# The end of a two-layer attention kernel: key sums on the matrix engine, an early start of the last projection, and a last part in four pieces

## The chip, the cores and the metric

The kernel runs on one core of a Trainium2 chip. The metric is the device time of one execution in microseconds. The kernel before takes 1591.75 us, the median of 3 runs (1589.45 to 1593.44). The engines are called as the profile calls them: PE (matrix multiply), DVE (vector), ACT (activation functions), POOL (GpSimd) and SP (which only issues DMAs).

## The reference

Two layers over 8 batches of 512 rows and 512 features. The first is a graph attention with 20 keys; it is finished before the part that this change touches. The second, cut to what matters:

```python
h = _sln(hidden, w, ...)                       # layer norm with learned gain and shift
qkv = (h @ Wqkv.T + bqkv)                      # 16 heads of 32 features
energy = jnp.einsum('bhqd,bhkd->bhqk', q, k)
att = jax.nn.softmax(energy, axis=-1) / D ** 0.5
out = jnp.einsum('bhqk,bhkd->bhqd', att, v)
out = out @ Wp.T + bp
h1 = out + hidden
h2 = _sln(h1, w, ...)
return h2 + h1
```

The softmax needs the sum of its exponentials over the keys (called key sum here). Since it is over keys, which lie on partitions, it is a sum across partitions.

## The kernel before

The second layer handles a batch in four units of four heads each; a unit is written (b, c) with b = 0..7 and c = 0..3, so the last two units are (7, 2) and (7, 3). A unit has 16 slots. In a slot PE writes one transposed score block of 128 keys by 512 queries (`scores_t`, L1407) into bank 0 or 1, ACT takes its exponential into the tile `pt` (`exp`, L1169), and PE may overwrite the bank two slots later. Beside it PE makes, in the same slot, the next unit's scores for the row maximum (L1420, with a DVE maximum behind it) and one piece of a projection: three matmuls of 512 columns (L48 to L50, `mm3`), which are the three products of a number split in a high and a low part. In the last unit there is no next unit and no projection, so its slots hold one matmul each.

`pt` holds four key chunks of four heads. The key sum is made in two steps. POOL adds the four chunks (`key_sum`, L1017 and L1022: six additions of 128x1024 for a unit) into `acc`, and PE multiplies `acc` with a tile of ones (`denominators`, L1455, four matmuls), which adds over the partitions and puts the sum on all 32 rows of a head (bank XB = 5). PE multiplies `pt` with the values in `weighted` (L1444, eight matmuls for two key chunks, twice per unit: at slot 14, and at slot 2 of the next unit; bank OB = 4). DVE takes the reciprocal of the sum in four pieces of 128 columns (`reciprocals`, L1295) and multiplies (`quotients`, L1302); ACT adds a bias and splits off the high part (`output_hi`, L1176 and L1179), POOL makes the low part (`output_lo`, L1036, into `ol`). `ol` of all four units is what the output projection of the batch needs (`output`, L48 to L50: 4 tiles of 128 rows by 4 pieces of contraction, one piece for each unit, three matmuls each). For batches 0 to 6 that projection lies in the next batch's slots. For batch 7 it stands after everything else, in banks 6, 7, 0 and 1. Behind it DVE adds the residual (L1381) and makes the statistics, POOL the reciprocal root (L1027, L1031), ACT the normalised tile (L1257), and DVE and POOL finish it (L1390, L1096, L1393); SP stores the four tiles.

The order on each engine is written out by hand; engines wait for each other through counting semaphores. POOL's order matters most here: between key sums it also makes `output_lo` and the results of the batch before (`result`, L1045 to L1049).

Of the kernel before, what the change touches and what calls it, by code (L numbers as in the profile page):

```python
# [847 lines left out]
def attention(nc, t, d):  # L848
# [12 lines left out]
    with ExitStack() as ctx:  # L861
# [70 lines left out]

        def last_tiles():

            return [(v[:, 0, i, :], pt[:, 0, i, :]) for i in range(NT)]
# [72 lines left out]
        def _(pool):  # L1008
# [42 lines left out]
            def batch(b, bpar, more):  # L1051
                later = not first(b)
                for c in range(FC):
                    if not start(b, c):
# [8 lines left out]
                    key_sum(b, c, 0, 1)  # L1063
                    key_sum(b, c, 0, 2)
# [4 lines left out]
                    key_sum(b, c, 1, 0)  # L1069
# [4 lines left out]
                    key_sum(b, c, 1, 1)  # L1074
                    if c == 2:
                        output_lo(b, 1)
# [9 lines left out]
            key_sum(B - 1, FC - 1, 1, 2)  # L1086
            output_lo(B - 1, FC - 1)
# [11 lines left out]
        def _(act):  # L1099
# [56 lines left out]
            def exp(b, c, slot):  # L1156
                G = 4 * b + c
                half, i, k = slot // 8, slot % 8 // 2, slot % 2
                if k == 0 and not start(b, c):
                    if i == 0:  # L1160
                        act.wait_ge(s["pv_done"], 2 * G - 1)
                        act.wait_ge(s["sum_done"], 6 * G + 3 * half - 5)
                    if i == 2:
                        act.wait_ge(s["pv_done"], 2 * G)
                        act.wait_ge(s["sum_done"], 6 * G + 3 * half - 4)
                    if i == 3:
                        act.wait_ge(s["sum_done"], 6 * G + 3 * half - 3)
# [86 lines left out]
            output_hi(B - 1, FC - 1)  # L1254
# [6 lines left out]
        def _(dve):  # L1261
# [26 lines left out]
            def reciprocals(b, c, piece):  # L1288
# [6 lines left out]
                nc.vector.reciprocal(rden[:, c % 2, col], bank[:, XB, col]).then_inc(s["rden_done"], 1)  # L1295
# [77 lines left out]
            for piece in range(4):  # L1373
                reciprocals(B - 1, FC - 1, piece)
            quotients(B - 1, FC - 1)
            hy = last_tiles()
            dve.wait_ge(s["h4_in"], 16)
            for i in range(NT + 2):
                if i < NT:
                    dve.wait_ge(s["pj_ready"], 4 * (B - 1) + i + 1)  # L1380
                    nc.vector.tensor_tensor(hy[i][0], bank[:, (QB, KB, 0, 1)[i], :], hy[i][0], ALU.add).then_inc(s["h1_done"], 1)  # L1381
# [14 lines left out]
        def _(pe):  # L1396
# [37 lines left out]
            def weighted(b, vpar, c, part):  # L1434
# [5 lines left out]
                if c == 0:  # L1440
                    pe.wait_ge(s["v_done"], 4 * b + 2 + 2 * part)
                for i in (2 * part, 2 * part + 1):
# [76 lines left out]

            def piece(b, c, slot, more):  # L1520
# [23 lines left out]
            def batch(b, bpar, more):  # L1544
                for c in range(FC):
                    former = None if start(b, c) else ((b, bpar, c - 1) if c else (b - 1, 1 - bpar, 3))
                    following = c < 3 or more
                    for slot in range(SLOTS):
# [8 lines left out]
                        if slot == 4 and former:  # L1557
                            denominators(former[0], former[2])
# [141 lines left out]
```

## Time and profile before

| | |
|---|---|
| time, median of 3 runs | 1591.75 us |
| time of the profiled execution | 1588.15 us |
| its span, first to last instruction | 1586.4 us |
| PE busy | 1376.4 us (87%) |
| DVE busy | 923.2 us (58%) |
| POOL busy | 899.5 us (57%) |
| ACT busy | 631.1 us (40%) |
| mean granted PE clock | 0.927 |

Busy time is the sum of an engine's instructions; the span is what one execution lasts on the core, and 1.75 us more lie around it. The granted clock is a share of 2.4 GHz; it is 1.0 or 0.5 (1.2 GHz) at any time, and a mean between them says how long each lasted. The last unit's first slot starts at 1525.47 us and the last DVE instruction ends at 1583.85 us.

### The profile page before, as it was taken

The page shows a single profiled execution, that of the slowest core. Times are in us where ns is not written, and L with a number is a line of the kernel's source. Part 1 is how long each engine was busy: PE and PEld are TensorE (multiplying, and loading weights), DVE is VectorE, ACT ScalarE, POOL GpSimd, SP SyncE. Part 2 cuts the span into 40 slices and gives each one's busy share as a digit, 9 for nine tenths or more (in the row PEclk, how much of TensorE's full clock was granted, in tenths as well). Part 3 has the DMA queues.
Part 4 walks back from the last instruction along what each step waited for, and adds up shares of the span by engine and source line. Part 5 has one row for each costly group of instructions (what it writes and reads, how often), then busy time and mean ns, then how long its engine had stood idle before and what let it go on. Part 6 is the DMA issues. An engine that isn't in the chain of part 4 may idle for free.

```text
span 1586.4 us, 19843 instructions
## 1 busy us (share of the span) xinstructions
PE 1376.4 (87%) x5988; PEld 873.2 (55%) x5988; DVE 923.2 (58%) x1494; ACT 631.1 (40%) x1090; POOL 899.5 (57%) x568
## 2 busy tenths in 40 slices
PE   6986998898898995279999999999999999999974
PEld 3644665665665663155565656555556555656532
DVE  2541665665664755136566757576667566666744
ACT  0231323324334232315454545545545445454551
POOL 1004434545545524316466958778769578687793
PEclk9997899999998987579999999999999999999977
DMA  9454213333323212724224425344344244253310
GB/s 297 177 174 129 83 65 132 136 113 135 125 106 153 86 60 106 265 73 109 73 61 127 114 61 147 94 107 108 87 127 111 62 127 111 70 143 89 104 46 27
DMA packets 107192, 179.41 MB, mean 113 GB/s; under 512 B 41312, under 2 KB 50848, under 8 KB 101840
## 3 DMA queue, kind: packets, MB, share of 16 engines
q1 hardware_dynamic: 94976, 143.92, 29.5%
q10 hardware_dynamic: 12112, 34.24, 7.2%
q8 instruction: 49, 0.80, 0.2%
q14 instruction: 55, 0.45, 0.1%
HBM read 81.06 MB, written 46.17 MB: 80 GB/s over the span
## 4 chain that ended last, share of the span: by engine, by line
PE 19%; POOL 17%; issue 8%; DVE 8%; ACT 3%; DMA 1%; SPq 1%; ACTq 1%; POOLq 0%; DVEq 0%
POOL acc L1022 7%; PE a_bank L1444 4%; PE a_bank L1407 4%; DVE rden L1295 4%; POOL acc L1017 3%; PE a_bank L1420 3%; PE a_bank L48 2%; PE a_bank L49 2%; PE a_bank L50 2%; DVE mx L1277 2%; PE a_bank L1455 2%; POOL h L1046 2%; POOL tn L1045 2%; ACT pt L1169 1%; DMA pt<-in_wp_t 1%
## 5 line engine op out<-in xcount | busy, mean ns | idle before, releaser
L1277 DVE TENSOR_REDUCE mx<-a_bank 128x1 f32<-128x512 f32 x512 | 341.9, 674 | 275.0 <-PE a_bank L1420 273.3
L1169 ACT ACTIVATE pt<-a_bank 128x512 f32<-128x512 f32 x512 | 301.9, 597 | 380.6 <-PE a_bank L1407 354.7
L1022 POOL TENSOR_TENSOR acc<-acc,pt 128x1024 f32<-128x1024 f32 x128 | 305.1, 2384 | 18.1 <-ACT pt L1169 9.9
L1407 PE MATMUL a_bank<-sq_stack,sk_stack 98*128 98x512 f32 x512 | 227.6, 447 | 31.1 <-ACT pt L1169 15.1
L1420 PE MATMUL a_bank<-sk_stack,sq_stack 96*128 96x512 f32 x512 | 220.0, 433 | 21.0 <-DVE mx L1277 19.7
L1017 POOL TENSOR_TENSOR acc<-pt 128x1024 f32<-128x1024 f32 x64 | 152.7, 2386 | 117.4 <-PE a_bank L1455 77.4
L1407 PEld LDWEIGHTS a_bank<-sq_stack,sk_stack 98*128 98x128 f32 x512 | 98.6, 193 | 158.3 <-issue 97.7
L774 PE MATMUL g_bank<-m,sf 128*128 128x320 f32 x512 | 161.9, 461 | 1.9 <-issue 1.9
L1420 PEld LDWEIGHTS a_bank<-sk_stack,sq_stack 96*128 96x128 f32 x512 | 99.9, 195 | 68.7 <-DVE mx L1277 54.6
L1295 DVE RECIPROCAL rden<-a_bank 128x128 f32<-128x128 f32 x128 | 120.1, 942 | 20.2 <-PE a_bank L1455 20.2
L48 PE MATMUL a_bank<-hh,wqkh 128*128 128x512 f32 x256 | 104.4, 408 | 27.5 <-DVE wqkl L1365 27.5
L1444 PE MATMUL a_bank<-pt,v 128*32 128x512 f32 x1024 | 126.6, 613 | 0.7 <-ACT pt L1169 0.7
L774 PEld LDWEIGHTS g_bank<-m,sf 128*128 128x128 f32 x512 | 97.0, 199 | 45.0 <-issue 15.7
L49 PE MATMUL a_bank<-hl,wqkh 128*128 128x512 f32 x256 | 103.5, 404 | 0.0
L50 PE MATMUL a_bank<-hh,wqkl 128*128 128x512 f32 x256 | 102.7, 401 | 0.0
L494 POOL TENSOR_TENSOR e<-e,cadd 128x640 f32<-128x640 f32 x32 | 49.4, 1543 | 92.0 <-DVE e L667 92.0
L479 POOL TENSOR_TENSOR xl<-xraw,xh 128x512 fp32r<-128x512 f32 x32 | 40.1, 1267 | 70.0 <-ACT xh L550 61.8
L689 DVE TENSOR_TENSOR wtl<-g_bank,wth 80x512 fp32r<-80x512 f32 x64 | 43.3, 685 | 57.8 <-ACT wth L583 57.4
L48 PE MATMUL g_bank<-wth,vdiag 80*128 80x512 f32 x64 | 40.1, 627 | 41.1 <-DVE wtl L689 41.0
L667 DVE TENSOR_TENSOR e<-g_bank,mask 128x640 f32<-128x640 f32 x32 | 26.4, 824 | 84.5 <-PE g_bank L776 84.5
L48 PEld LDWEIGHTS a_bank<-hh,wqkh 128*128 128x128 f32 x256 | 49.9, 195 | 39.3 <-DVE wqkl L1365 27.9
L566 ACT ACTIVATE ln<-xn,nmr,rstd 128x512 f32<-128x512 f32 x32 | 23.4, 802 | 120.7 <-DVE nmr L719 120.7
(164 smaller groups left out, 2540.6 us busy)
## 6 DMA issues: line engine op xcount, KB each, us to landing
sq_stack<-qh SPq DMA_DIRECT2D x256, 64.0 KB, 2.0
sk_stack<-kh SPq DMA_DIRECT2D x256, 64.0 KB, 2.3
m_rows<-mout SPq DMA_DIRECT2D x8, 1280.0 KB, 5.0
m<-m_rows SPq DMA_DIRECT2D x8, 1280.0 KB, 5.7
xraw<-in_x_t SPq DMA_DIRECT2D x8, 1024.0 KB, 7.5
xn<-in_x SPq DMA_DIRECT2D x8, 1024.0 KB, 6.8
h_rows<-xn ACTq DMA_DIRECT2D x8, 1024.0 KB, 3.9
t_rows<-houth SPq DMA_DIRECT2D x8, 1024.0 KB, 3.9
```

Source lines behind the costliest of these rows:

```text
L48: nc.tensor.matmul(out, ah, bh, start=start, stop=False)
L49: nc.tensor.matmul(out, ah, bl, start=False, stop=False)
L50: return nc.tensor.matmul(out, al, bh, start=False, stop=stop)
L774: nc.tensor.matmul(out, sf2[:, par, f, i * P:(i + 1) * P], m[:, f, dr, :], start=f == 0, stop=False)
L1017: nc.gpsimd.tensor_tensor(acc[:, two, :], pt[:, 0, two, :], pt[:, 1, two, :], ALU.add).then_inc(s["sum_done"], 1)
L1022: nc.gpsimd.tensor_tensor(acc[:, two, :], acc[:, two, :], pt[:, step + 1, two, :], ALU.add).then_inc(s["sum_done"], 1)
L1169: nc.scalar.activation(pt[:, i, 2 * half + k, :], bank[:, k, :], ACT.Exp).then_inc(s["exp_done"], 1)
L1277: nc.vector.reduce_max(mx[:, half, k, n:n + 1], bank[:, 2 + e % 2, :], AX).then_inc(s["emax_done"], 1)
L1295: nc.vector.reciprocal(rden[:, c % 2, col], bank[:, XB, col]).then_inc(s["rden_done"], 1)
L1407: nc.tensor.matmul(bank[:, k, :], sk[0:3 * DH + 2, c % 2, j, i * P:(i + 1) * P], sq[0:3 * DH + 2, c % 2, j, :], start=True, stop=True).the ...
L1420: nc.tensor.matmul(bank[:, 2 + e % 2, :], sq[0:3 * DH, c % 2, j, n * P:(n + 1) * P], sk[0:3 * DH, c % 2, j, :], start=True, stop=True).the ...
L1444: last = nc.tensor.matmul(bank[DH * j:DH * j + DH, OB, :], v[:, vpar, i, (HC * c + j) * DH:(HC * c + j + 1) * DH], pt[:, i, j, :], start=i ...
```

## The change

There are three parts, and all lie in units (7, 2) and (7, 3) and in what follows them.

1. For the last two units POOL makes no key sums. PE multiplies every chunk of `pt` with the ones, right ahead of each `weighted` part: eight matmuls of 32 rows by 512 for each part, four parts. The sum of (7, 2) goes to bank KB = 7, that of (7, 3) to XB. The waits of `exp` for those sums go too.
2. Of the last projection the pieces of units (7, 0), (7, 1) and (7, 2), twelve of sixteen, are put in slots 3 to 14 of the last unit, in banks 6, 2, 3 and 7. Four pieces, those of (7, 3), are left for the end.
3. What follows the last `weighted` goes in pieces of 128 columns (128 output rows): reciprocal, product, the two activations and the low part, and each piece releases one tile's last three matmuls.

```diff
+        def final(b, c):
+            return isinstance(b, int) and b == B - 1 and c >= 2
+        END = (QB, 2, 3, KB)
...
-                    key_sum(b, c, 0, 0)
+                    if not final(b, c):
+                        key_sum(b, c, 0, 0)
...
-            key_sum(B - 1, FC - 1, 1, 2)
-            output_lo(B - 1, FC - 1)
+            for p in range(NT):
+                col = slice(p * P, (p + 1) * P)
+                pool.wait_ge(s["ob_done"], 4 * B + p)
+                nc.gpsimd.tensor_tensor(ol[:, FC - 1, col], rden[:, 1, col], oh[:, FC - 1, col].bitcast(F32),
+                                        ALU.subtract).then_inc(s["ol_done"], 1)
...
-            output_hi(B - 1, FC - 1)
+            for p in range(NT):
+                n, col = 4 * B + p, slice(p * P, (p + 1) * P)
+                act.wait_ge(s["o_done"], n)
+                nc.scalar.activation(oh[:, FC - 1, col], rden[:, 1, col], ACT.Identity,
+                                     bias=bvs[:, FC - 1:FC]).then_inc(s["oh_done"], 1)
+                act.wait_ge(s["oh_done"], n)
+                nc.scalar.activation(rden[:, 1, col], rden[:, 1, col], ACT.Identity,
+                                     bias=bvs[:, FC - 1:FC]).then_inc(s["ob_done"], 1)
...
-            for piece in range(4):
-                reciprocals(B - 1, FC - 1, piece)
-            quotients(B - 1, FC - 1)
+            for p in range(NT):
+                col = slice(p * P, (p + 1) * P)
+                reciprocals(B - 1, FC - 1, p)
+                if p == 0:
+                    dve.wait_ge(s["pv_done"], 8 * B)
+                dve.wait_ge(s["rden_done"], 16 * (B - 1) + 12 + p + 1)
+                nc.vector.scalar_tensor_tensor(rden[:, 1, col], bank[:, OB, col], float(D) ** -0.5, rden[:, 1, col],
+                                               ALU.mult, ALU.mult).then_inc(s["o_done"], 1)
...
+                if final(b, c):
...
+                    for i in (2 * part, 2 * part + 1):
+                        for j in range(HC):
+                            last = nc.tensor.matmul(bank[DH * j:DH * j + DH, KB if c == 2 else XB, :], ones32[:, :],
+                                                    pt[:, i, j, :], start=i == 0, stop=i == NT - 1)
+                    if part == 1:
+                        last.then_inc(s["den_ready"], 1)
...
+            early = {3: (0, 0), 4: (1, 0), 5: (2, 0), 6: (0, 1), 7: (1, 1), 8: (2, 1), 9: (3, 0), 10: (3, 1),
+                     11: (0, 2), 12: (1, 2), 13: (2, 2), 14: (3, 2)}
...
+                if final(b, c) and c == 3 and slot in early:
+                    i, f = early[slot]
+                    if f == 0:
+                        pe.wait_ge(*((s["h1_done"], 4 * b), (s["emax_done"], SLOTS * FC * B), (s["emax_done"], SLOTS * FC * B),
+                                     (s["rden_done"], 4 * (4 * b + c)))[i])
+                    output(b, i, END[i], f)
...
-            denominators(B - 1, FC - 1)
-            pe.wait_ge(s["h1_done"], 4 * (B - 1))
             for i in range(NT):
-                for f in range(FC):
-                    output(B - 1, i, (QB, KB, 0, 1)[i], f)
+                pe.wait_ge(s["ol_done"], 4 * B + i)
+                output(B - 1, i, END[i], FC - 1)
```

The order on PE in the last unit. This is the kernel before, from slot 3 of unit (7, 3) on; L1407 is a slot's score block, L1455 the key sum of (7, 2) from `acc`, L1444 the first `weighted` part of (7, 3):

```order
L1407 MATMUL a_bank<-sq_stack,sk_stack 128x512 [waits exp_done] x2
L1455 MATMUL a_bank<-acc,ones 32x512 [waits sh_lo,sum_done]
L1455 MATMUL a_bank<-acc,ones 32x512 x3
L1407 MATMUL a_bank<-sq_stack,sk_stack 128x512 [waits exp_done] x3
L1407 MATMUL a_bank<-sq_stack,sk_stack 128x512 [waits exp_done,shrow_lo,shrow_hi]
L1407 MATMUL a_bank<-sq_stack,sk_stack 128x512 [waits exp_done] x6
L1444 MATMUL a_bank<-pt,v 32x512 [waits o_done,exp_done]
```

The changed kernel on PE, from slot 10 to the first part of the key sums and the weighted sum of (7, 3); L1435 is now the score block, L48 to L50 a projection piece, L1478 the ones-matmuls, L1484 `weighted`:

```order
L48 MATMUL a_bank<-wph,oh 128x512 [waits ol_done]
L49 MATMUL a_bank<-wpl,oh 128x512
L50 MATMUL a_bank<-wph,ol 128x512
L1435 MATMUL a_bank<-sq_stack,sk_stack 128x512 [waits exp_done]
L48 MATMUL a_bank<-wph,oh 128x512
L49 MATMUL a_bank<-wpl,oh 128x512
L50 MATMUL a_bank<-wph,ol 128x512
L1435 MATMUL a_bank<-sq_stack,sk_stack 128x512 [waits exp_done]
L48 MATMUL a_bank<-wph,oh 128x512
L49 MATMUL a_bank<-wpl,oh 128x512
L50 MATMUL a_bank<-wph,ol 128x512
```

Each slot from 3 to 14 now holds four matmuls where it held one, and the first piece above, in slot 11, waits for `ol_done`, the low part of unit (7, 2).

DVE at the end of the kernel before, from the last unit's reciprocals to the first residual:

```order
L1295 RECIPROCAL rden<-a_bank 128x128 [waits ol_done,den_ready]
L1295 RECIPROCAL rden<-a_bank 128x128 x3
L1302 SCALAR_TENSOR_TENSOR rden<-a_bank,rden 128x512 [waits rden_done,pv_done]
L1381 TENSOR_TENSOR v<-a_bank,v 128x512 [waits pj_ready,h4_in]
L1315 BN_STATS stat<-v 128x6 [waits h1_done]
```

The same place in the changed kernel (L1317 the reciprocal, L1402 the product of 128 columns, L1409 the residual):

```order
L1317 RECIPROCAL rden<-a_bank 128x128 [waits ol_done,den_ready]
L1402 SCALAR_TENSOR_TENSOR rden<-a_bank,rden 128x128 [waits rden_done,pv_done]
L1317 RECIPROCAL rden<-a_bank 128x128
L1402 SCALAR_TENSOR_TENSOR rden<-a_bank,rden 128x128 [waits rden_done]
L1317 RECIPROCAL rden<-a_bank 128x128
L1402 SCALAR_TENSOR_TENSOR rden<-a_bank,rden 128x128 [waits rden_done]
L1317 RECIPROCAL rden<-a_bank 128x128
L1402 SCALAR_TENSOR_TENSOR rden<-a_bank,rden 128x128 [waits rden_done]
L1409 TENSOR_TENSOR v<-a_bank,v 128x512 [waits pj_ready,h4_in]
```

Reciprocals and products alternate now, and all eight stand ahead of the first residual in DVE's queue.

## Rows read from the trace of the kernel before

**Rows 1.** Busy time of PE, PEld, DVE, ACT, POOL; then granted clock, DMA.

```profile
1522.30:1584.00 61.70, 36.96 (x149) 17.70 (x149) 26.34 (x48) 19.86 (x34) 39.72 (x31) 0.76 0.09 30
```

**Rows 2.** The chain that ended last, from 1530 us: start, us, what.

```profile
1530.50 2.34 POOL acc L1022
...
1550.20 2.35 POOL acc L1022
...
1552.59 1.11 PE a_bank L1455 x8
...
1553.73 3.40 DVE rden L1295 x4
...
1557.22 0.70 DVE rden L1302
...
1557.95 0.73 ACT oh L1176
...
1559.50 1.27 POOL ol L1036
```

**Rows 3.** Timeline of PE, units (7, 2) and (7, 3): start, us, instruction, idle before.

```profile
1519.68 0.47 PE L1407 MATMUL a_bank<-sq_stack,sk_stack 98*128 98x512 f32 x1
...
1520.92 0.39 PE L1407 MATMUL a_bank<-sq_stack,sk_stack 98*128 98x512 f32 x1
...
1523.04 1.92 PE L1444 MATMUL a_bank<-pt,v 128*32 128x512 f32 x16
...
1529.33 0.73 PE L1407 MATMUL a_bank<-sq_stack,sk_stack 98*128 98x512 f32 x2
1532.89 1.55 PE L1455 MATMUL a_bank<-acc,ones 128*32 128x512 f32 x8 [2.83 <-POOL acc L1022]
...
1542.51 3.64 PE L1444 MATMUL a_bank<-pt,v 128*32 128x512 f32 x16
...
1547.56 1.92 PE L1444 MATMUL a_bank<-pt,v 128*32 128x512 f32 x16 [0.69 <-ACT pt L1169]
```

**Rows 4.** Stretches as in Rows 1: PE waits, and what follows them.

```profile
1071.60:1074.00 2.40, 0.07 (x2) 0.04 (x1) 0.09 (x1) 0.00 (x0) 2.32 (x2) 1.00 0.80 229
1074.00:1080.00 6.00, 6.00 (x34) 3.49 (x35) 3.25 (x5) 2.64 (x5) 0.94 (x1) 1.00 0.55 140
1287.40:1290.00 2.60, 0.05 (x1) 0.08 (x1) 0.00 (x0) 0.00 (x0) 2.52 (x2) 1.00 0.76 218
1291.10:1294.40 3.30, 3.30 (x10) 2.42 (x9) 1.68 (x3) 0.95 (x3) 0.00 (x0) 0.50 0.69 188
1510.10:1512.90 2.80, 0.04 (x1) 0.00 (x0) 2.80 (x5) 1.25 (x3) 2.66 (x3) 0.99 0.17 64
1513.00:1519.60 6.60, 6.51 (x15) 4.91 (x16) 3.79 (x6) 2.22 (x4) 6.46 (x5) 0.50 0.17 46
...
1533.40:1546.90 13.50, 11.97 (x35) 3.68 (x27) 4.08 (x5) 6.92 (x12) 13.07 (x8) 0.50 0.19 58
```

**Rows 5.** Timeline of DVE after the last projection has begun.

```profile
1562.57 0.69 DVE L1381 TENSOR_TENSOR v<-a_bank,v 128x512 f32<-128x512 f32 x1 [4.66 <-PE a_bank L50]
...
1564.32 0.14 DVE L1322 TENSOR_SCALAR stat<-stat 128x1 f32<-128x1 f32 x1
...
1568.77 0.69 DVE L1381 TENSOR_TENSOR v<-a_bank,v 128x512 f32<-128x512 f32 x1 [0.83 <-PE a_bank L50]
...
1583.16 0.69 DVE L1393 TENSOR_TENSOR v<-v,pt 128x512 f32<-128x512 f32 x1
```

**Rows 6.** Groups by line and form: xcount, busy us, mean ns, idle before.

```profile
L1169 ACT ACTIVATE pt<-a_bank 128x512 f32<-128x512 f32 x512 | 301.9, 597 | 380.6 <-PE a_bank L1407 354.7 <-POOL acc L1022 15.1 <-issue 7.2
L152 ACT ACTIVATE ident<-ident_raw 128x128 fp32r<-128x128 f32 x1 | 0.3, 310 | 3.0 <-DMA bbias<-in_b_bias 3.0
L1285 DVE SCALAR_TENSOR_TENSOR sht<-a_bank,sht 8x128 fp32r<-8x128 f32 x64 | 17.4, 272 | 7.6 <-ACT sht L1151 7.6
L1022 POOL TENSOR_TENSOR acc<-acc,pt 128x1024 f32<-128x1024 f32 x128 | 305.1, 2384 | 18.1 <-ACT pt L1169 9.9
```

More of the change, by code:

```diff
@@ L1053, in batch @@
                 for c in range(FC):
-                    if not start(b, c):
+                    if not start(b, c) and not final(b, c - 1):
                         key_sum(*(ahead(b, c, -1) if c else (b - 1, 3)), 1, 2)
@@ L1059, in batch @@
                         result(b - 1, 2 * c - 3)
-                    key_sum(b, c, 0, 0)
+                    if not final(b, c):
+                        key_sum(b, c, 0, 0)
                     if later and c in (1, 2):
                         result(b - 1, 2 * c - 2)
-                    key_sum(b, c, 0, 1)
-                    key_sum(b, c, 0, 2)
+                    if not final(b, c):
+                        key_sum(b, c, 0, 1)
+                        key_sum(b, c, 0, 2)
                     if c == 0 and later:
@@ L1068, in batch @@
                         output_lo(b, 2)
-                    key_sum(b, c, 1, 0)
+                    if not final(b, c):
+                        key_sum(b, c, 1, 0)
                     if c == 2:
@@ L1073, in batch @@
                         rsqrt(b - 1, 2 * c - 1)
-                    key_sum(b, c, 1, 1)
+                    if not final(b, c):
+                        key_sum(b, c, 1, 1)
                     if c == 2:
@@ L1161, in exp @@
                         act.wait_ge(s["pv_done"], 2 * G - 1)
-                        act.wait_ge(s["sum_done"], 6 * G + 3 * half - 5)
                     if i == 2:
                         act.wait_ge(s["pv_done"], 2 * G)
+                    if i == 0 and not final(b, c - 1):
+                        act.wait_ge(s["sum_done"], 6 * G + 3 * half - 5)
+                    if i == 2 and not final(b, c - 1):
                         act.wait_ge(s["sum_done"], 6 * G + 3 * half - 4)
-                    if i == 3:
+                    if i == 3 and not final(b, c - 1):
                         act.wait_ge(s["sum_done"], 6 * G + 3 * half - 3)
@@ L1294, in reciprocals @@
                         dve.wait_ge(s["ol_done"], G - 1)
-                nc.vector.reciprocal(rden[:, c % 2, col], bank[:, XB, col]).then_inc(s["rden_done"], 1)
+                nc.vector.reciprocal(rden[:, c % 2, col], bank[:, KB if final(b, c) and c == 2 else XB, col]
+                                     ).then_inc(s["rden_done"], 1)
             def quotients(b, c):
@@ L1380, in _ @@
                     dve.wait_ge(s["pj_ready"], 4 * (B - 1) + i + 1)
-                    nc.vector.tensor_tensor(hy[i][0], bank[:, (QB, KB, 0, 1)[i], :], hy[i][0], ALU.add).then_inc(s["h1_done"], 1)
+                    nc.vector.tensor_tensor(hy[i][0], bank[:, END[i], :], hy[i][0], ALU.add).then_inc(s["h1_done"], 1)
                     statistics(B - 1, i, hy[i][0])
@@ L1441, in weighted @@
                     pe.wait_ge(s["v_done"], 4 * b + 2 + 2 * part)
+                if final(b, c):
+                    if part == 0 and c == 2:
+                        pe.wait_ge(s["h1_done"], 4 * b - 1)
+                    if part == 0 and c == 3:
+                        pe.wait_ge(s["sh_lo"], 2 * FC * B)
+                        pe.wait_ge(s["rden_done"], 4 * (G - 1))
+                    for i in (2 * part, 2 * part + 1):
[4 more added lines that the diff above has]
+                        last.then_inc(s["den_ready"], 1)
                 for i in (2 * part, 2 * part + 1):
@@ L1556, in batch @@
                             weighted(*former, 1)
-                        if slot == 4 and former:
+                        if slot == 4 and former and not final(b, c - 1):
                             denominators(former[0], former[2])
```

## The prediction, made before the changed kernel was run

> **What bounds the end now.** The change touches nothing ahead of the end of unit (7, 2), so I read only the last 63 us. First the stretch from 1522.3 us, where the two kernels part, to the last DVE instruction: POOL is busy 39.72 of 61.70 us, PE 36.96, DVE 26.34 and ACT 19.86 [rows 1]. No engine is full, so a chain decides. The chain of waits says which: from 1530.50 to 1552.55 us it is POOL alone, addition after addition of key sums, with the batch's other POOL work between them; then the sum on PE (1.11 us), four reciprocals (3.40), the product (0.70), two activations (1557.95 to 1559.43), the low part (1.27), and at 1560.82 the first matmul that could finish a tile [rows 2]. PE had done the last `weighted` by 1549.48 and stands still for 3.1 us until the sum is there; at 1530.06 it had stood still for 2.83 us for the sum of (7, 2) [rows 3]. Then comes a tail of DVE: the first residual starts at 1562.57, the third at 1568.77, the last instruction ends at 1583.85 [rows 5].
>
> So the time from 1522.3 us is POOL's chain, a serial hand-over of 13.1 us (1549.48 to 1562.57), and a tail of 21.3 us.
>
> **What the change takes away.** Twelve POOL additions of 2.38 us [rows 6], 28.6 us, leave the queue, nine of them (21.4) in this stretch; eight `acc` matmuls leave PE. POOL keeps some 18 us of work for 62 us [rows 1, 6] and no longer bounds. What is late next is PE, whose queue I replay in order at the full clock. Four blocks are what matters.
>
> (a) *To slot 3 of the last unit.* Each `weighted` part took 1.86 us at full clock (1.92 with its drain) for eight matmuls that fill 32 of 128 columns [rows 3]. The ones-matmuls have the same form and moving data, so eight cost 1.86 again. Bounds: nothing, if they overlapped `weighted` wholly (eight more instructions of one form in one queue; the row shows no such slack), and 3.64 at the half clock [rows 3]. I take 1.86. Two such blocks lie ahead of slot 3, which moves from 1529.33 to 1533.05. The exponential of slot 15 comes later, but waits beside the blocks.
>
> (b) *Slots 3 to 10.* A slot with five matmuls took 1.24 us at full clock (1519.68 to 1520.92) [rows 3], 0.248 each. Four are 0.99. Slot s + 2 needs the exponential of slot s: 0.5 for the matmul and 0.6 on ACT [rows 6], 1.2 in two slots of 1.98, so PE bounds and not ACT. Eight slots are 7.9 us; slot 11's score block starts at 1540.95.
>
> (c) *A new stall in slot 11.* Its piece waits for the low part of unit (7, 2), which ACT begins only behind the exponential of slot 10. That slot's matmul starts at 1539.97; + 0.5 + 0.6 + hand-over = 1541.15; two activations 1.5, low part 1.27, hand-overs 0.1 [rows 2]: 1544.0. PE has nothing from 1541.2 on: 2.8 us idle. Behind the waiting piece stand slots 12 to 14 and both last `weighted` parts, and ACT waits for those slots.
>
> (d) *To the end of the last `weighted`.* Three matmuls and three slots, 0.7 + 2.97 = 3.7: 1547.7. Ones and `weighted` 3.72: 1551.4. Slot 15, its exponential and hand-over 1.2 [rows 3, 6]: 1552.6. Ones and `weighted` 3.72: X = 1556.35. Before it was 1549.48, so PE's part costs 6.9 us more.
>
> (e) *From X to the first residual.* The ones-matmuls end 1.9 us before X, so the first reciprocal is done. Then DVE has four products and three reciprocals in its queue ahead of the first residual. A reciprocal is 0.85 back to back (3.40 for four [rows 2]), 0.95 alone here. A product of 128 columns is not in the trace: between 0.27 (8x128 [rows 6]) and 0.70 (128x512 [rows 2]); I take 0.3, nearest to the 128-column row. 4 x 0.3 + 3 x 0.9 = 3.9, with hand-over X + 4.0. Tile 0 is ready by then: product 0.3, two activations of 128 columns (0.31 each [rows 6], at most 0.73 [rows 2]), low part 0.45 (the line through 1.27 at 512 columns and 2.38 at 1024; at most 1.27), three matmuls 1.0, or 1.7 at the half clock: X + 2.6 to X + 3.3. The other tiles follow every 1.2 us, sooner than DVE can take them. All costs of pieces but the product's are hidden behind DVE's queue; with the product at its upper bound 1.7 us are lost. So 13.1 us of hand-over become 4.0: 9.1 us saved.
>
> (f) *The tail.* Before, the third tile came from PE 6.2 us after the first [rows 5]. Now it is DVE that sets it: a tile's residual and statistics take 1.9 (1562.57 to 1564.46 [rows 5]), two tiles 3.85. From the third residual on everything is as before, 15.08 us [rows 5]. The tail is 18.9 in place of 21.3: 2.4 saved.
>
> **Sum at full clock:** + 6.9 - 9.1 - 2.4 = - 4.6 us.
>
> **The clock.** PE's idle stretches are what this sum has not priced. After 2.8 us of idle at 1510.1 the clock was 0.50 for 6.6 us of dense work; after 2.6 at 1287.4 it was 0.50 for 3.3; after 2.4 at 1071.6 it stayed 1.00; after the 2.83 at 1530.1 it was 0.50 for 13.5 us, of which 11.97 busy, in lone score matmuls with waits between [rows 3, 4]. The stall in (c) is 2.8, so I expect a fall. Each us of low clock in PE-bound work costs 0.5. Dense work follows, so I take a low stretch of 3.4 us: 1.7 lost. Both ends: 0 and 3.3 (6.6 us low). Before, a low clock in the last unit cost nothing, since POOL bounded.
>
> The Trainium skill, TensorE: Matmul & The Clock Gate, section Loop structure matters more than you think, says that a loop which waits between its matmul bursts brings PE back to the slow clock. By that rule the stall of (c) always costs and the sum with it is the forecast; by the 2.4 us row alone it might not, and the sum is the 4.6.
>
> **Forecast:** - 4.6 + 1.7 = - 2.9 us. The profiled execution took 1588.15 (span 1586.4 and 1.75 around it), 3.6 below the median; a difference carries over: 1591.75 - 2.9 = 1588.9 us, a span near 1583.5 in an execution like the profiled one.
>
> **Rivals.**
> - *No fall of the clock.* The stall is a little shorter than I count, or straddles as that of 2.4 us did. - 4.6, and up to 0.4 more if slot 15's wait hides in (a): 1587.1. For it: one of the four stretches. Against: the three others, each 2.6 or longer.
> - *Long low clock after the stall.* As at 1513.0 [rows 4], 6.6 us: - 4.6 + 3.3 = - 1.3, 1590.4. If the product also costs its upper bound, 0.4 slower, 1592.2. Either reads as no change.
> - *Slower: the last unit runs at the half clock.* The clock falls in the sparse slots 15, 0, 1 and 2 or is low as it is before, and stays low through slots 3 to 14, as it did for 13.5 us [rows 4]. PE now bounds there, with 7.9 + 3.7 us of work that doubles: - 4.6 + 11.6 = + 7.0, 1598.8. It decides from 9.2 us of low clock on, where the gain is gone. Against: that stretch had waits in every slot, while four matmuls a slot are dense work, and dense work brought the clock back in 3.3 and 6.6 us.
> - *The change doesn't do what it says*: POOL's chain could still be last if `output_lo` of (7, 2) were behind late results. With 18 us of work left in 62 [rows 1, 6], POOL is idle when that low part comes; no chance of its own.
>
> **Chances.** Forecast 0.42, no fall 0.35, long low 0.12, slower 0.09, others 0.02. What a measurement can tell is 0.3%, 4.8 us. The no-fall case reaches it in half of its share, the forecast in a sixth, with the error of a median of a few runs: faster 0.27. Slower 0.10, no change that can be told 0.63. The range: the low end 1585.0 is the no-fall case less 2 for the error of the replay and of medians. The high end 1594.0 takes in the long low clock with the dear product and the same error; beyond it lies most of the slower case. The forecast's own range is 1586.5 to 1591.3.
>
> **What would show it.** Right: no L1022 after 1505 us; ones-matmuls 1.9 us per part; a slot of about 1.0 us in the last unit at clock 1.0; an idle stretch of 2.8 us in front of slot 11's piece, released by POOL's low part, and a clock of 0.50 behind it; the last `weighted` ending 6 to 9 us later than 1549.5; the first residual 4 us after it; DVE without waits for PE from there on. Wrong: ones-matmuls that cost other than `weighted`; slots set by ACT; a first residual that waits for PE or POOL; a low clock ahead of slot 10; a tail that is not 18.9 us.

## The result: 7.65 us faster, where 2.9 were forecast

The changed kernel takes 1581.80 us (median of 11 runs, 1577.84 to 1589.21), the kernel before 1589.45 (11 runs, 1585.98 to 1595.05; the 1591.75 from which I had worked was a median of three). The ratio is 0.995, 95% interval 0.993 to 0.9969: faster by 5 to 11 us. The direction was right. The size was not: the forecast was 1588.9, with a range from 1585.0 to 1594.0.

The profiled execution took 1580.23 us. Its page, with the busy time of the engines and three of the groups:

```profile
span 1578.3 us, 19927 instructions
...
PE 1372.0 (87%) x6036; PEld 872.2 (55%) x6036; DVE 923.1 (58%) x1497; ACT 633.7 (40%) x1096; POOL 872.0 (55%) x559
...
L1028 POOL TENSOR_TENSOR acc<-acc,pt 128x1024 f32<-128x1024 f32 x120 | 286.1, 2384 | 17.4 <-ACT pt L1184 9.8
...
L1023 POOL TENSOR_TENSOR acc<-pt 128x1024 f32<-128x1024 f32 x60 | 143.3, 2388 | 120.4 <-PE a_bank L1495 79.9
```

Eight additions of L1028 (L1022 before, [rows 6]) and four of L1023 are gone, and POOL is busy 27.5 us less. POOL's busy time isn't the gain; the gain is read from the end of the span. The timeline of PE in units (7, 2) and (7, 3), to be read beside [rows 3] (start, us, instruction, idle before it):

```profile
1519.57 1.92 PE L1478 MATMUL a_bank<-pt,ones 128*32 128x512 f32 x16
1521.31 1.90 PE L1484 MATMUL a_bank<-pt,v 128*32 128x512 f32 x16
...
1528.84 0.50 PE L1435 MATMUL a_bank<-sq_stack,sk_stack 98*128 98x512 f32 x1
1529.88 0.40 PE L1435 MATMUL a_bank<-sq_stack,sk_stack 98*128 98x512 f32 x1
...
1535.47 0.40 PE L1435 MATMUL a_bank<-sq_stack,sk_stack 98*128 98x512 f32 x1
...
1536.41 0.39 PE L1435 MATMUL a_bank<-sq_stack,sk_stack 98*128 98x512 f32 x1
1539.26 0.61 PE L48 MATMUL a_bank<-wph,oh 128*128 128x512 f32 x1 [2.46 <-POOL ol L1042]
...
1549.25 1.92 PE L1478 MATMUL a_bank<-pt,ones 128*32 128x512 f32 x16 [0.69 <-ACT pt L1184]
1550.99 1.90 PE L1484 MATMUL a_bank<-pt,v 128*32 128x512 f32 x16
1554.80 0.47 PE L48 MATMUL a_bank<-wph,oh 128*128 128x512 f32 x1 [1.90 <-POOL ol L1099]
```

The reader sees the new ones block (L1478) ahead of `weighted` (L1484), slots of one score matmul and three of the projection, 0.93 us apart, and in slot 11 the new stall, released by POOL's low part of (7, 2). The granted clock through it, as windows with the columns of [rows 1]:

```profile
1519.50:1536.80 17.30, 17.07 (x104) 8.98 (x103) 7.34 (x14) 11.16 (x20) 7.02 (x7) 1.00 0.19 62
1536.90:1539.20 2.30, 0.00 (x0) 0.00 (x0) 0.00 (x0) 1.42 (x3) 1.26 (x1) 1.00 0.00 0
1539.50:1542.80 3.30, 3.30 (x9) 2.52 (x9) 0.00 (x0) 0.60 (x1) 0.00 (x0) 0.50 0.00 0
1542.90:1554.00 11.10, 9.30 (x72) 3.08 (x71) 2.00 (x3) 2.47 (x5) 0.00 (x0) 1.00 0.01 1
1557.20:1560.00 2.80, 2.80 (x6) 1.64 (x6) 2.63 (x8) 0.85 (x3) 1.20 (x3) 0.50 0.00 0
```

PE is full up to slot 10, empty for 2.3 us, and then full at half the clock for 3.3 us. The chain of waits through the stall (start, us, what):

```profile
1535.91 0.60 ACT pt L1184
1536.51 0.62 ACT oh L1191
1537.14 0.73 ACT rden L1194
...
1537.94 1.27 POOL ol L1042
1539.26 0.61 PE a_bank L48
```

POOL's additions of key sums, which filled this stretch of the chain before [rows 2], have gone, and one low part is left. After the last `weighted` part DVE alone sets the pace up to the third residual, to be read beside [rows 5]:

```profile
1552.96 0.29 DVE L1402 SCALAR_TENSOR_TENSOR rden<-a_bank,rden 128x128 f32<-128x128 f32 x1 [0.76 <-PE a_bank L1484]
...
1554.15 0.29 DVE L1402 SCALAR_TENSOR_TENSOR rden<-a_bank,rden 128x128 f32<-128x128 f32 x1
...
1556.73 0.68 DVE L1409 TENSOR_TENSOR v<-a_bank,v 128x512 f32<-128x512 f32 x1
...
1560.31 0.68 DVE L1409 TENSOR_TENSOR v<-a_bank,v 128x512 f32<-128x512 f32 x1
...
1574.86 0.69 DVE L1421 TENSOR_TENSOR v<-v,pt 128x512 f32<-128x512 f32 x1
```

No residual (L1409) waits for PE any more. From such timelines I split every profile in the same way. F is the start of the first ones or `weighted` block in slot 14 of unit (7, 2); X the end of the last `weighted` part; R1 and R3 the starts of the first and third residual; E the end of the last DVE instruction. F to E is called the end stretch below. All in us:

| kernel | F at | F to X | X to R1 | R1 to R3 | R3 to E | end stretch |
|---|---|---|---|---|---|---|
| before | 1523.04 | 26.44 | 13.09 | 6.20 | 15.08 | 60.81 |
| before, second profile (`e5_same`) | 1522.63 | 26.77 | 13.51 | 7.26 | 15.08 | 62.62 |
| changed | 1519.57 | 33.32 | 3.84 | 3.58 | 15.24 | 55.98 |
| changed, second profile (`e9_changed_again`) | 1526.28 | 33.34 | 3.84 | 3.58 | 15.25 | 56.01 |
| `e1_ones` | 1521.34 | 27.52 | 6.58 | 6.98 | 15.08 | 56.16 |
| `e2_pieces` | 1524.86 | 26.77 | 9.28 | 4.83 | 15.25 | 56.13 |
| `e3_no_early` | 1523.45 | 28.33 | 3.84 | 4.61 | 15.26 | 52.04 |
| `e4_no_stall` | 1521.80 | 29.29 | 3.85 | 3.58 | 15.24 | 51.96 |
| `e6_tail` | 1523.68 | 34.63 | 3.84 | 3.58 | 11.65 | 53.70 |
| `e10_half_again` | 1523.26 | 25.65 | 3.84 | 3.59 | 15.24 | 48.32 |
| `e8_best` | 1526.11 | 24.77 | 3.85 | 3.58 | 11.64 | 43.84 |
| `e11_best_no_early` | 1523.80 | 25.93 | 3.85 | 4.60 | 11.46 | 45.84 |

The column F at has to be read with care. It lies between 1519.57 and 1526.28 us, though the instructions ahead of it are the same but for POOL's key sums of (7, 2), and the two ends of the range are the same kernel twice. One profile's span is therefore no measure of this change, and the end stretch is. Each end stretch here is of one execution; the kernel before and the changed one have two.

### The profile page after: what moved, and what is told of

The parts are those of the page before. It is cut to its first block, busy times and chain, and to the rows that moved or that the text cites. A ratio compares the mean times of both kernels' runs of the same rounds, so it can differ in the third digit from the quotient of the medians.

```text
span 1578.3 us, 19927 instructions
## 1 busy us (share of the span) xinstructions
PE 1372.0 (87%) x6036; PEld 872.2 (55%) x6036; DVE 923.1 (58%) x1497; ACT 633.7 (40%) x1096; POOL 872.0 (55%) x559
## 4 chain that ended last, share of the span: by engine, by line
PE 20%; POOL 16%; DVE 8%; issue 8%; ACT 3%; DMA 2%; SPq 1%; ACTq 1%; POOLq 0%; DVEq 0%
POOL acc L1028 7%; PE a_bank L1484 4%; PE a_bank L1435 4%; DVE rden L1317 4%; POOL acc L1023 3%; PE a_bank L1448 3%; PE a_bank L48 2%; PE a_bank L49 2%; PE a_bank L50 2%; DVE mx L1299 2%; POOL h L1052 2%; POOL tn L1051 2%; PE a_bank L1495 1%; ACT pt L1184 1%; DMA pt<-in_wp_t 1%
## 5 line engine op out<-in xcount | busy, mean ns | idle before, releaser
L1028 POOL TENSOR_TENSOR acc<-acc,pt 128x1024 f32<-128x1024 f32 x120 | 286.1, 2384 | 17.4 <-ACT pt L1184 9.8
L1435 PE MATMUL a_bank<-sq_stack,sk_stack 98*128 98x512 f32 x512 | 225.7, 441 | 31.2 <-ACT pt L1184 15.7
L1023 POOL TENSOR_TENSOR acc<-pt 128x1024 f32<-128x1024 f32 x60 | 143.3, 2388 | 120.4 <-PE a_bank L1495 79.9
L1435 PEld LDWEIGHTS a_bank<-sq_stack,sk_stack 98*128 98x128 f32 x512 | 97.9, 191 | 153.3 <-issue 96.3
L774 PE MATMUL g_bank<-m,sf 128*128 128x320 f32 x512 | 158.5, 454 | 1.9 <-issue 1.9
L1317 DVE RECIPROCAL rden<-a_bank 128x128 f32<-128x128 f32 x128 | 120.3, 942 | 19.9 <-PE a_bank L1478 19.8
L48 PE MATMUL a_bank<-hh,wqkh 128*128 128x512 f32 x256 | 104.1, 407 | 27.4 <-DVE wqkl L1388 27.4
L1484 PE MATMUL a_bank<-pt,v 128*32 128x512 f32 x1024 | 124.6, 605 | 0.0
L50 PE MATMUL a_bank<-hh,wqkl 128*128 128x512 f32 x256 | 102.5, 400 | 0.0
L48 PE MATMUL g_bank<-wth,vdiag 80*128 80x512 f32 x64 | 40.5, 633 | 40.4 <-DVE wtl L689 40.2
L48 PEld LDWEIGHTS a_bank<-hh,wqkh 128*128 128x128 f32 x256 | 50.0, 195 | 39.1 <-DVE wqkl L1388 27.8
```

The lines of the kernel that those rows point to most:

```text
L48: nc.tensor.matmul(out, ah, bh, start=start, stop=False)
L50: return nc.tensor.matmul(out, al, bh, start=False, stop=stop)
L774: nc.tensor.matmul(out, sf2[:, par, f, i * P:(i + 1) * P], m[:, f, dr, :], start=f == 0, stop=False)
L1023: nc.gpsimd.tensor_tensor(acc[:, two, :], pt[:, 0, two, :], pt[:, 1, two, :], ALU.add).then_inc(s["sum_done"], 1)
L1028: nc.gpsimd.tensor_tensor(acc[:, two, :], acc[:, two, :], pt[:, step + 1, two, :], ALU.add).then_inc(s["sum_done"], 1)
L1317: nc.vector.reciprocal(rden[:, c % 2, col], bank[:, KB if final(b, c) and c == 2 else XB, col]).then_inc(s["rden_done"], 1)
```

## Experiments

Two theories stood against each other after the result. A: the gain arises in the end stretch, as the prediction has it, with terms mis-sized. B: a good part of it arises ahead of F, where F had come 3.5 us earlier in the changed kernel's profile.

### Each part alone

`e1_ones` has part 1 only (ones-matmuls on every chunk), on the changed kernel:

```diff
-            early = {3: (0, 0), 4: (1, 0), ... 14: (3, 2)}
+            early = {}
 # ACT, POOL and DVE end with whole output_hi, output_lo, reciprocals, quotients again
 # PE: all sixteen pieces behind the last weighted
```

> Part 1 alone: ones-matmuls for the last two units, the projection whole at the end, the hand-over in whole tiles. The measure is the end stretch: from the first block of weighted or ones-matmuls in slot 14 of (7,2) to the end of the last DVE instruction; 60.8 us in the kernel before, 56.0 in the changed one. Theory A (a replay of the queues: POOL's chain goes, slots are then set by the matmul-exponential loop, 0.62 us each, and the early projection fills PE beyond what the slots leave free): the last weighted ends 26 to 28 us into the stretch in place of 33.3 in the changed kernel, the hand-over takes 6.3, the tail 21.3; end stretch 54 to 56, that is 5 to 7 us under before. Theory B (the early projection carries the gain): this alone saves no more than 2 us, end stretch 58 or more.

Measured: 1584.06 us against 1589.71 for the kernel before measured beside it (ratio 0.9966, interval 0.9942 to 0.999); end stretch 56.16. It falls just above the 54 to 56 that was expected. The ones save by themselves 4.65 us of the 60.81. R1 follows X by 6.58 instead of 13.09, since the wait of 3.11 us for POOL's sum [rows 2, 3] is gone, and the reciprocals start 1.65 us ahead of X (1547.21) and not 4.25 behind it.

`e2_pieces` has part 3 only, on the kernel before: POOL makes the key sums as before, and the end goes in pieces of 128 columns.

```diff
-            output_hi(B - 1, FC - 1)
+            for p in range(NT):
 # as in the change, on ACT, POOL and DVE; PE's piece f == 3 of tile i waits for ol_done 4 * B + i
```

> Part 3 alone, on the kernel before: key sums by POOL, projection at the end, the hand-over in pieces of 128 columns. Both theories: the last weighted ends at 26.4 us as before, 3.1 us wait for the key sum, four reciprocals and products ahead of the first residual. Hand-over from the key sum on 4.8 in place of 8.9 us, tail still set by PE: end stretch 56 to 57.5, 3.5 to 4.5 us under before. If the pieces were worth something only with the early projection: 60 or more.

Measured: 1585.25 (0.997, 0.9949 to 0.9991); end stretch 56.13, as expected. So parts 1 and 3 save 4.7 us each against the first profile of before, and together they should be able to save nearly twice that. The changed kernel, which has both, saves 4.83.

### Without the early start

`e3_no_early` leaves out part 2 alone:

```diff
-            early = {3: (0, 0), 4: (1, 0), ... 14: (3, 2)}
+            early = {}
...
+            pe.wait_ge(s["h1_done"], 4 * (B - 1))
             for i in range(NT):
-                pe.wait_ge(s["ol_done"], 4 * B + i)
-                output(B - 1, i, END[i], FC - 1)
+                for f in range(FC):
+                    if f == FC - 1:
+                        pe.wait_ge(s["ol_done"], 4 * B + i)
+                    output(B - 1, i, END[i], f)
```

> Parts 1 and 3 without part 2: no projection piece in the last unit's slots, all sixteen behind the last weighted, tile by tile. Theory A: slots of 0.62 us, no stall in slot 11, last weighted ends 26 to 28 us into the stretch; hand-over 4.0; the third tile is ready 8.8 us after the last weighted and not 7.7: end stretch 26.5 + 8.8 + 15.1 = 50.4, plus up to 3 us for a low clock in the tail: 50.5 to 53.5, 2.5 to 5.5 us faster than the changed kernel. Theory B: the early pieces save what they do at the end, 12 x 0.7 = 8.3 us: end stretch 58 or more, slower than the changed kernel.

Measured: 1579.35 (0.9934, 0.9914 to 0.9955); end stretch 52.04, 3.9 less than the changed kernel. Part 2, the early start of the projection, makes the end slower. The medians point the same way (2.4 us), but their intervals overlap, so the profiles carry this. PE's timeline of this kernel shows the price of thin slots beside it:

```profile
1535.13 3.49 PE L1435 MATMUL a_bank<-sq_stack,sk_stack 98*128 98x512 f32 x6 [0.19 <-ACT pt L1184]
...
1541.18 3.64 PE L1478 MATMUL a_bank<-pt,ones 128*32 128x512 f32 x16
...
1548.14 1.92 PE L1478 MATMUL a_bank<-pt,ones 128*32 128x512 f32 x16 [0.69 <-ACT pt L1184]
```

Here x6 are the score matmuls of six slots. They take 3.5 us, 0.6 each, which is the exponential's 597 ns [rows 6]; four matmuls in a slot take 0.93. But the ones block at 1541.18 takes 3.64 where the later one takes 1.92: the clock was low.

```profile
1539.20:1545.90 6.70, 5.93 (x26) 1.76 (x30) 0.00 (x0) 2.29 (x5) 1.27 (x1) 0.52 0.00 0
```

### Without the stall

`e4_no_stall` keeps all three parts and moves ACT's two activations of (7, 2) four slots up, so that the low part is there before slot 11:

```diff
-                            if c == 3:
+                            if c == 3 and more:
                                 output_hi(b, 2)
+                        if slot == 6 and c == 3 and not more:
+                            output_hi(b, 2)
```

> The changed kernel with the activations of (7,2) behind the exponential of slot 6 in place of slot 10, so that its low part is there when slot 11's piece wants it. Theory A: no idle stretch of 2.8 us in slot 11, and so no low clock behind it: end stretch 56.0 - 2.5 - 1.6 = 52 us (53.5 if the clock falls elsewhere). Rival (the stall is hidden behind ACT or DVE anyway): 55.5 to 56, the wait only moves to another slot.

Measured: 1579.04 (0.9938, 0.9916 to 0.9959); end stretch 51.96. The stall and its low clock cost the changed kernel 4.02 us, against 4.5 forecast (2.8 idle and 1.7 of clock). The window from F to behind X (at 1551.09) shows PE busy for 29.42 of 32.30 us and the clock whole:

```profile
1521.70:1554.00 32.30, 29.42 (x187) 14.28 (x186) 11.14 (x21) 16.73 (x31) 9.17 (x10) 1.00 0.11 34
```

It ends where `e3_no_early` ends: twelve early pieces, with the stall cured, are worth nothing. F to X is 0.96 us longer than without them, and R1 to R3 1.03 us shorter. What they save after X lay behind DVE's queue but for that 1.03. What they cost ahead of X is time in the slots: from slot 3's score matmul to the ones block of slot 14 it is 11.62 us (1531.08 to 1542.70) where `e3_no_early` takes 8.42 (1532.76 to 1541.18), 3.2 more. The two blocks behind it take 2.2 us longer in `e3_no_early`, at its low clock, and that is why only 1.0 is left.

### The same kernels again

`e5_same` is the kernel before, unchanged.

> The kernel before, unchanged: what the measurement shows between two equal kernels, and a second profile of it. The stretch ahead of the last units started within 5.3 us of each other in six kernels with the same code there. Theory A (those differences, and about 3 us of the 7.7 by which the medians of before and after differ, are the spread of one execution to the next, where the clock falls in other places): ratio 1.000 within 0.003, span anywhere in 1581 to 1590, end stretch 60 to 63. Theory B (the change also makes the part ahead of slot 14 of (7,2) faster): this kernel reaches that slot later than the changed one in every profile, at 1523 us or more, and its stretch from slot 8 to slot 14 of (7,2) lasts 9.7 to 10 us as in the two kernels with POOL's key sums, in place of the 8.5 of the four with ones-matmuls.

Measured: 1589.80 (1.0009, 0.9992 to 1.0027), as theory A has it. From slot 8 to F it took 9.64 us (1512.99 to 1522.63), close to theory B's 9.7 to 10. Its end stretch is 62.62, 1.81 more than in the first profile. F to X and X to R1 hold 0.75 of that, R1 to R3 1.06. The reason for most of it stands in a window on the projection, here and then in the first profile of the kernel before:

```profile
1560.30:1566.50 6.20, 5.34 (x13) 4.18 (x14) 1.78 (x5) 0.70 (x1) 1.54 (x3) 0.50 0.01 3
```

```profile
1560.70:1564.00 3.30, 3.18 (x8) 2.51 (x9) 1.39 (x2) 0.00 (x0) 0.06 (x1) 0.50 0.02 5
```

The low clock lasted 6.2 us instead of 3.3, and the residuals, which wait for PE in this kernel, came later:

```profile
1562.91 0.69 DVE L1381 TENSOR_TENSOR v<-a_bank,v 128x512 f32<-128x512 f32 x1 [4.66 <-PE a_bank L50]
...
1570.17 0.69 DVE L1381 TENSOR_TENSOR v<-a_bank,v 128x512 f32<-128x512 f32 x1 [0.84 <-PE a_bank L50]
```

`e9_changed_again` is the changed kernel, unchanged.

> The changed kernel, unchanged, measured again beside the next two. Theory A (what its first comparison shows beyond the end stretch is spread): ratio between 0.9945 and 0.998, that is 3 to 9 us, its end stretch 54.3 to 57.5 by where the clock falls. Theory B (about 3 us are gained ahead of the end stretch): ratio 0.995 or less again, and slot 14 of (7,2) reached before 1521 us again.

Measured: 1581.78 (0.9953, 0.9936 to 0.997), end stretch 56.01. F was at 1526.28 instead of 1519.57, and the ratio is the same, so an early F is no mark of the changed kernel. What is left for theory B is the stretch from slot 8 to F. It took 9.64 to 9.95 us in all three profiles with POOL's key sums of (7, 2) (both of before, `e2_pieces`), and 8.5 in six and 9.5 to 9.7 in three of the nine with ones-matmuls. The means are 0.9 us apart; with three profiles against nine that can be chance, and no run decides it. The stall in slot 11 and the fall behind it are there again:

```profile
1543.40:1545.90 2.50, 0.12 (x1) 0.00 (x0) 0.00 (x0) 1.64 (x3) 1.24 (x1) 1.00 0.00 0
1546.60:1549.80 3.20, 3.20 (x9) 2.52 (x8) 0.00 (x0) 0.99 (x2) 0.00 (x0) 0.50 0.02 5
```

### The tail

`e6_tail` lets POOL do its addition for tile i - 1 right behind the root of tile i, where it was tile i - 2:

```diff
-            for i in range(NT + 2):
+            for i in range(NT + 1):
...
-                if i >= 2:
-                    y = hy[i - 2][0]
-                    pool.wait_ge(s["ln_done"], 4 * (B - 1) + i - 1)
+                if i >= 1:
+                    y = hy[i - 1][0]
+                    pool.wait_ge(s["ln_done"], 4 * (B - 1) + i)
```

> The changed kernel with POOL's additions in the tail one place earlier: tile 0's behind the root of tile 1 in place of tile 2, and so on. If the waits of DVE for POOL (two of 1.99 us in the tail) are on the path: from the third residual to the end 11.3 to 13.3 us in place of 15.2, end stretch 52.5 to 54. If the two engines then run into each other (the last product took 1.66 us beside POOL's additions and 0.69 without): 14 to 15, end stretch 55 or more.

Measured: 1580.92 (0.9943, 0.9926 to 0.996); end stretch 53.70. R3 to E falls from 15.24 to 11.65. The 3.6 us are not all seen in the end stretch, because in this execution the low clock after the stall of slot 11 lasted 6.2 us, from 1543.4 to 1549.6 by the length of its matmuls (0.63 instead of 0.40), where it had lasted 3.4: F to X is 34.63 instead of 33.32. The medians show little of the 3.6: 1580.92 against 1581.80 and 1581.78 for the changed kernel, differences that the intervals do not tell from 3.6 or from nothing.

### Better versions

`e7_half` starts six pieces early instead of twelve, one in every second slot, none of which needs (7, 2). That unit's activations go to slot 14, its first piece behind slot 15's score matmul, and the other nine pieces behind the last `weighted`.

```diff
-            early = {3: (0, 0), 4: (1, 0), ... 14: (3, 2)}
+            early = {3: (0, 0), 5: (0, 1), 7: (1, 0), 9: (1, 1), 11: (2, 0), 13: (2, 1)}
```

> Six of the twelve early pieces, in every second slot from 3 to 13; one piece behind slot 15's score block; the other five behind the last weighted and between the four last parts; the activations of (7,2) behind the exponential of slot 14. Theory A (a slot leaves PE 0.4 us free, so three matmuls in two slots cost nothing, and the hand-over of 2.2 us holds three pieces): last weighted 25 to 27 us into the stretch, hand-over and tail as in the changed kernel (22.7): end stretch 47.5 to 50, 6 to 8 us under the changed kernel and 2 to 4 under the one without early pieces. Rival (PE's clock falls in the thinner slots, 0.74 us a slot and 3.6 us blocks at half clock): 51 to 53.

Measured: 1575.74, the median of all 7 executions, or 1575.36 without the one that took 4452.93 us (0.991, 0.9886 to 0.9935). The profile is of that one and cannot be split. It is told of under the hardware below. `e10_half_again` is the same kernel, measured again.

> The kernel with six early pieces in every second slot, again, since one execution of its first measurement (the profiled one) ran with PE at a fraction of its speed from end to end. As then: end stretch 47.5 to 50 by theory A, 51 to 53 if the clock falls in the thin slots; ratio 0.990 to 0.993.

Measured: 1576.01 (6 runs; 0.9915, 0.9894 to 0.9936), the same time again, and an end stretch of 48.32. Theory A had 47.5 to 50. F to X is 25.65, the shortest so far and less than before the change, though it holds the ones blocks and half of the pieces.

`e8_best` adds the tail of `e6_tail`, lets slot 15's score matmul go ahead of the ones block of slot 14 in the last unit, puts ACT's two activations in slot 15, and moves the first piece of (7, 2) behind the last `weighted`.

```diff
-                        if slot == 14:
+                        if slot == (15 if final(b, c) and c == 3 else 14):
                             weighted(b, bpar, c, 0)
```

> As the one with six early pieces, and in addition: the first ones and weighted block of (7,3) behind slot 15's score block in place of slot 14's, so that the exponential of slot 15 runs beside it; the activations of (7,2) behind slot 15; POOL's additions in the tail one place earlier. Theory A: 0.7 us less for the block's place and 2 to 3.5 for the tail: end stretch 44 to 47.5, 13 to 17 us under the kernel before. If the tail gives nothing: 47 to 49.

Measured: 1570.05 (6 runs, 1567.66 to 1574.62; 0.988, 0.9856 to 0.9904), the fastest: 19 us under the kernel before measured beside it (1589.47). The end stretch is 43.84, just under the 44 to 47.5 that was expected. PE's timeline has matmuls in pairs and the two last blocks without a wait between:

```profile
1535.39 0.50 PE L1437 MATMUL a_bank<-sq_stack,sk_stack 98*128 98x512 f32 x1
...
1536.42 0.65 PE L1437 MATMUL a_bank<-sq_stack,sk_stack 98*128 98x512 f32 x2
...
1543.81 1.92 PE L1480 MATMUL a_bank<-pt,ones 128*32 128x512 f32 x16
...
1547.27 1.90 PE L1480 MATMUL a_bank<-pt,ones 128*32 128x512 f32 x16
1548.98 1.90 PE L1486 MATMUL a_bank<-pt,v 128*32 128x512 f32 x16
```

```profile
1526.10:1551.00 24.90, 24.67 (x167) 10.35 (x167) 8.31 (x16) 14.46 (x26) 8.31 (x8) 1.00 0.14 44
```

PE is busy 24.67 of 24.90 us at the full clock. `e11_best_no_early` asks whether the six pieces do anything: it is `e8_best` with `early = {}` and all pieces at the end.

> The best kernel so far (end stretch 43.8) without any piece in the last unit's slots; all sixteen behind the last weighted, tile by tile. What early pieces are worth once the slots are not PE's bound: theory A: a slot with one matmul is no shorter than one with two and a half (0.62 to 0.67), the third tile comes 8.8 us after the last weighted in place of 7.4: end stretch 44.5 to 46, 0.7 to 2 us worse; if the clock falls in the thin slots and PE's 48 matmuls at the end run at half clock, 48 to 51. Rival (early pieces worth nothing): 43.5 to 44.

Measured: 1576.22 (6 runs; 0.9913, 0.9888 to 0.9937), end stretch 45.84, 2.0 more. Its slots are thin again, and the clock fell in them:

```profile
1537.50:1543.90 6.40, 6.21 (x18) 2.09 (x22) 0.00 (x0) 5.18 (x9) 0.18 (x1) 0.51 0.11 38
```

Here the early pieces help, by 1.2 us from F to X and by 1.0 from R1 to R3. The medians say 6 us, but the two intervals overlap (0.9856 to 0.9904, 0.9888 to 0.9937), and the 2.0 is from one profile of each. That the pieces help is likely; how much stays open.

## Why the direction was right and the size was not

By the prediction's own steps:

**(a) to slot 3.** 9.27 us (1519.57 to 1528.84), forecast 10.01 (1523.04 to 1533.05). A ones block costs what a `weighted` part does: 1.74 from its start to the next block's, 1.92 with its drain. I had taken 1.86. Of the wait of 0.68 us for an exponential that stood in this stretch before, 0.23 are left; I had allowed that only in a rival. 0.74 too much.

**(b) slots 3 to 10.** 7.57 (1528.84 to 1536.41), 1.04 for the first slot and 0.93 to 0.94 for the others, forecast 7.9. I had divided a slot of five matmuls by five, 0.248, but a matmul in a row takes 0.233; the first of that slot had taken 0.32. 0.33 too much.

**(c) the stall.** It is there, in slot 11, released by POOL's low part and named ahead of time. From the score matmul of slot 10 (1535.47) to PE's next start (1539.26) it took 3.79, forecast 4.03; idle 2.46, forecast 2.8. 0.24 too much.

**The clock.** It fell in all three profiles of kernels with this stall (changed, `e9_changed_again`, `e6_tail`), for 3.4, 3.4 and 6.2 us of PE's work. The first two are the forecast's case: F to X is 4.03 us longer than in `e4_no_stall`, of which the idle is 2.46 and the clock about 1.6, forecast 1.7. `e6_tail` is the rival of a long low clock, and its F to X is 1.3 us longer again. The rival without a fall had 0.35, and none of the three shows it. The Trainium skill says that a loop which waits for a DMA between its matmuls brings the slow clock back (TensorE: Matmul & The Clock Gate, Loop structure matters more than you think). The windows agree in that the clock was 0.50 behind each of the three waits of 2.46 us in slot 11; the page's example waits 8 us each time, and behind the 2.4 us at 1071.6 us of the kernel before the clock stayed 1.00 [rows 4].

**(d) to the last `weighted`.** 13.63 from the end of the stall to X, forecast 12.35 + 1.7. 0.42 too much. With (a) to (c), F to X is 33.32 instead of 35.0: 6.9 us more than before, where 8.6 were forecast with the clock in. That the prediction has 6.9 too, at the full clock, is chance: the measured 6.9 holds 1.6 us of clock, which the 1.7 us too much in (a) to (d) make up for.

**(e) the hand-over.** 3.84, forecast 4.0. Product of 128 columns 0.29 (forecast 0.3), low part 0.45 (0.45), activation 0.40 (0.31, hidden). That DVE's queue hides all the costs of pieces but the product's was right.

**(f) the tail.** 18.82 (3.58 + 15.24), forecast 18.9 (3.85 + 15.08): a tile's residual and statistics take 1.79 and not 1.9, and the rest is 0.16 longer.

**The sum** of the end stretch is 60.81 - 55.98 = 4.83 against the first profile of before, forecast 2.9: the 1.9 us are 1.7 of (a) to (d), every one on the same side, and 0.2 of (e) and (f).

**The step that failed** is the term that I put at nothing, together with the reading of the kernel before from one execution. I wrote that before, a low clock in the last unit cost nothing, since POOL bounded. That holds for the unit but not for the projection behind it. The 13.1 us of hand-over and the 6.2 us from the first to the third residual, which (e) and (f) take away, hold a low clock whose length I took as fixed. PE enters there from a wait of 3.31 us for POOL's low part, at the low clock, and DVE waits for its matmuls:

```profile
1560.82 0.80 PE L48 MATMUL a_bank<-wph,oh 128*128 128x512 f32 x1 [3.31 <-POOL ol L1036]
```

In that execution it was 3.3 us. `e5_same` shows 6.2 and an end stretch 1.8 us longer. The changed kernel's projection also falls to 0.50 (1557.2 to 1560.0), but its residuals no longer wait for PE and R1 to R3 is 3.58 in both profiles. So against the one profile the change saves 4.8 us, against the other 6.6. What I let carry over was the smaller of the two. The changed kernel has a low clock of two lengths as well, behind its stall: by `e6_tail` the long one would add 1.3 us and bring the range to 3.5 to 6.6.

**The rest.** The medians differ by 7.65 us, and by 7.5 going by `e9_changed_again`'s ratio; the end stretches by 4.8 and 6.6. The 1 to 4 us between are inside the interval (0.9936 to 0.997 is 4.8 to 10.2 us) and inside the scatter of F, and remain open: no run located them. Of the 7.1 us by which the forecast missed the median, 2.3 are the old median of three runs, 1.9 the mis-sized terms, and the remaining 2.9 hold the low clock in the projection of before, up to 1.8, and what stays open.

Every execution's mean granted clock is on record, and it bears on this. Twice its distance from 1.0, times the span, is the time at the low clock. It is 231 us in the mean of the 73 executions of the kernel before that stand beside the experiments, and 214 and 216 us in the two sets of the changed one. The end stretches alone have 30 and 33 us of it before (0.75 of 60.81, 0.74 of 62.62) and 19 and 16 after (0.83 of 55.98, 0.86 of 56.01). So most of the 16 us of low clock that the change removes lie in the end stretch, and little is left for a gain ahead of F.

**What the prediction did not ask** is what each part is worth. By one profile each, parts 1 and 3 save 4.7 and part 2 loses 3.9: four matmuls in a slot make PE the bound (0.93 against 0.6), and a piece stands in the queue 2.5 us before its low part is there. This was written in (b) and (c) as a cost, but I had not set it against what part 2 saves, which (e) already said is hidden.

## What to carry to other kernels

Work that is moved into another loop's slots should fill what the bounding engine leaves, and no more. Here ACT's 0.6 us a slot leaves room for three matmuls in every second slot. With nothing beside the one score matmul the clock fell, and four in a slot make PE the bound. Before moving work ahead, look for the latest product that it reads, and place it behind that; `e4_no_stall` and `e10_half_again` gained 4.0 and 7.7 us by order alone. And measure the end that a change touches from a mark just ahead of it, in two profiles of each kernel. Here that mark shifted by 7 us between two executions of one kernel, and the terms worked out here are smaller.

## What the runs showed of the hardware

- **The clock fell around every stall of some 3 us, and stayed low for one of two times.** In all 12 profiles of the table PE stands idle for 2.94 to 2.97 us ahead of slot 8 of unit (7, 2). Read in windows of 0.1 us, the granted clock is then 0.50 for 3.4 us in six of them and for 6.8 or 6.9 in the other six. When it fell tells the two apart: in the six long ones it fell 0.2 to 1.2 us before PE started again, in the six short ones when PE started or up to 1.5 us later. The three stalls in slot 11 divide in the same way (3.4 us twice, 6.9 in `e6_tail`). The low clock in the first profile's last projection does not: it fell 0.2 us before PE's start and lasted 3.5. A short case (changed) and a long one (`e9_changed_again`), each by its first matmul behind the wait and a window:

```profile
1511.08 0.47 PE L1435 MATMUL a_bank<-sq_stack,sk_stack 98*128 98x512 f32 x1 [2.95 <-ACT pt L1184]
1511.10:1512.20 1.10, 1.10 (x5) 0.97 (x6) 0.46 (x2) 0.86 (x2) 1.10 (x2) 0.99 0.02 6
...
1516.59 0.77 PE L1435 MATMUL a_bank<-sq_stack,sk_stack 98*128 98x512 f32 x1 [2.97 <-ACT pt L1184]
1515.80:1516.60 0.80, 0.01 (x1) 0.04 (x1) 0.80 (x2) 0.80 (x3) 0.56 (x1) 0.50 0.83 317
```

  Slot 8 to F takes 8.5 us with the short one and 9.5 to 9.95 with the long one, and this is a part of the scatter of F.
- **The clock fell in thin slots.** With one matmul in a slot it fell to 0.50 in `e1_ones`, `e3_no_early` and `e11_best_no_early`, 4 to 6 us after slot 3, and stayed there for 6.8 us. With three projection matmuls in every second slot (`e8_best`, `e10_half_again`) it was 1.00 through the whole unit.
- **One execution of `e7_half` took 4452.93 us.** The granted clock was 1.00, PE was busy 4359.4 us (98%), and its matmuls were long: the score group, of which the changed kernel's page has 441 ns, had 1097.

```profile
L1437 PE MATMUL a_bank<-sq_stack,sk_stack 98*128 98x512 f32 x512 | 560.1, 1097 | 2.8 <-DMA sq_stack<-sht 2.8
```

  The same kernel took 1576.01 us again later, so it isn't the kernel. What it was stays open.
